# A two-layer graph kernel on one core: VectorE operands placed in PSUM, part of the last product moved into the node blocks

## The chip, the cores and the metric

The kernel runs on one core of a Trainium2 chip. The metric is the device time of the whole program in microseconds, lower is better. The core's engines are TensorE (PE, with its weight loads shown apart as PEld), VectorE (DVE), ScalarE (ACT), GpSimd (POOL) and SyncE (SP), and 16 DMA engines that they share. SBUF and PSUM are the two on-chip memories of 128 partitions; PE writes to PSUM, of which there are eight banks of 512 fp32 words per partition.

## The reference

Two message-passing layers over 6250 nodes of 160 features (64 scalars and 32 vectors of three) and 100,000 edges, all in fp32.

Layer 0 normalises the node rows (layer norm, then ReLU), gathers the row of the source of each edge, forms products with the four numbers of the edge, adds them up per node, and then forms in each node a full tensor product of the node's row with its sum (`uvw` products of 64x64x64, 64x32x32, 32x64x32 and 32x32x64) and a linear map; the input is added back. That gives y. Layer 1 normalises y again to h2, and does

```python
out_s = (einsum('eu,uo->eo', xs_e * es[:, None], W_ss) / sqrt(MUL_S) + einsum('eud,ed,uo->eo', xv_e, ev, W_vv) * ISQ3 / sqrt(MUL_V)) * ISQ2
out_v = (einsum('eu,ed,uv->evd', xs_e, ev, W_sv) * ISQ3 / sqrt(MUL_S) + einsum('eud,e,uv->evd', xv_e, es, W_vs) * ISQ3 / sqrt(MUL_V)) * ISQ2
messages = messages * sigmoid(edge_scalars @ W_rad.T + b_rad)
agg = segment_sum(messages, dst, num_segments=n)
h = x + agg
ys, yv = hs @ L_s / sqrt(MUL_S), einsum('nud,uv->nvd', hv, L_v) / sqrt(MUL_V)
```

with h2 as x, and the output is y plus this. The last product is linear, so the product of x + agg is that of x plus that of agg.

## The kernel before

Nodes are cut into NB = 49 blocks of 128. Edges are sorted by the block of their target, on the chip, and padded to windows of 256; two windows make a pair, and there are PAIRS = 220 pairs in each layer.

- **Ranks (VectorE, `ranks`, L506).** For each layer, keys are counted per block and given a place in the sorted order by a scan (L548, its first operand the constant `ones` in SBUF) and a predicated copy (L553) per block and part of the columns. The positions go to HBM. Between the two layers' ranks VectorE normalises the nodes (L580 to L599; `mean` and `rstd` are in SBUF).
- **Scatters (POOL, `scatter`, L408).** 782 indirect DMAs for each layer (L415) write the edges' records to their sorted places. SP loads pieces of records for layer 0, POOL itself for layer 1 (L425, L426).
- **Edges of layer 0.** POOL gathers the rows of a pair by four indirect DMAs (L449 into `xu`), up to five pairs ahead. ScalarE makes the keys (`dist`, L933) and scales the rows (L945). VectorE multiplies the rows with the edge's vector (L646, operand from `rw0` in SBUF), builds the one-hot matrices (`one_hot`, L617, from `iota` and `keyp` in SBUF), and adds the two sums of the pair before to the accumulator (L634). PE forms the sums (L1163).
- **Node blocks.** 49 blocks; VectorE forms the products (L728, L739, L747, L756, L762), PE turns them (`turn`, L1118, and L1230) and multiplies with the weights. For each block y is finished (L680 to L687), stored to `x2D` by SP (L350), normalised to `hb` (L707, L710), turned, copied to `hS` (L990), and `rows` (L1200) makes the table rows of layer 1 by two matmuls (L1202, L1203), which ScalarE copies (`copy_rows`) and SP stores. `rows(b-1)` stands in block b's program between the third and the fourth product of the turned blocks. POOL's scatters of layer 1 run beside this stage.
- **Edges of layer 1.** POOL gathers rows of 352 words (L449 into `tb`). VectorE: L858 (rows times the edge's vector, from `rw1`), L617, L865 (a sum over three), L827 (add of the sums of three pairs back), L833, L839, L827, L845 (messages times the gate `gt`). ScalarE: attributes (L1060), keys (L1063), L1082, the sigmoid (L1087, from PSUM to `gt`), scales (L1073). PE: flips (L1114), the gate's product (L1344), the sums (L1324).
- **Output (`output_pairs`, L240).** 49 blocks in turn, two in flight: VectorE adds the accumulator and `hS` (L897), PE flips the sum (L1114, `flip` is a matmul with the identity, `turn` a transpose) and forms the product (L1356, L1357), ScalarE copies, VectorE adds the row of x2 that SP has loaded (L893), SP stores 80 KB (L398).

The order on each engine is written out; loops run over pairs and over blocks, and engines wait for one another by counting semaphores.

## Time and profile before

| | us |
|---|---|
| median of 3 runs | 5143.87 |
| lowest and highest | 5098.26, 5165.8 |
| the profiled execution | 5144.9 |
| its span in the profile | 5143.2 |

| engine | busy us | share of the span |
|---|---|---|
| POOL | 3622.3 | 70% |
| DVE | 3371.4 | 66% |
| PE | 3032.4 | 59% |
| ACT | 1538.0 | 30% |

Shares are over stages that have different limits, so they don't say which engine sets the end. A row of the group view reads: line, engine, operation, output<-input by the program's names, partitions x elements, count | busy us, mean ns of one | idle time of the engine just before them, and what ended it. "issue" is time in which the engine waited for nothing that the profile shows. PEclk is the clock that TensorE was granted, as a share of 2.4 GHz; 0.5 is 1.2 GHz. In names, `acc` stands for all buffers that are cut from one large SBUF tile, and `ps` for PSUM.

### The profile page before, as it was taken

To read this page: it belongs to the slowest core of one execution; us is meant where nothing else is said; L and a number is where in the kernel's file an instruction comes from. 1 tells how busy PE (TensorE), PEld (TensorE's weight loads), DVE (VectorE), ACT (ScalarE), POOL (GpSimd) and SP (SyncE) were. 2 spreads that over 40 slices of the span, in tenths; PEclk is the share of its full clock that TensorE was granted. 3 is DMA by queue.
4 is the path that set the end of the run, shared out by engine and by line. 5 is a ranking of instruction groups with operands and counts; after the bars stand their busy time and mean duration, and the time that the engine had idled before them with its cause. 6 is when DMAs were issued, how large, how long until landed. Compare 5 with 4: busy or idle time off the path is not lost.

```text
span 5143.2 us, 56705 instructions
## 1 busy us (share of the span) xinstructions
PE 3032.4 (59%) x14598; PEld 1860.4 (36%) x14598; DVE 3371.4 (66%) x5385; ACT 1538.0 (30%) x4652; POOL 3622.3 (70%) x3420
## 2 busy tenths in 40 slices
PE   0030000005777777767888888888776677777779
PEld 0030000002222222224666656566544444444445
DVE  9959800005555555547999999999777677676751
ACT  0000000002333333333333333333254555554531
POOL 0787777777777777776777777777277777777740
PEclk9999999999999999999889999999799989899875
DMA  5020000003333333362111111111155555555571
GB/s 197 7 61 7 7 7 7 7 11 89 104 104 104 103 105 104 104 93 54 33 32 33 31 35 31 34 33 32 34 138 137 135 138 139 139 136 136 139 98 55
DMA packets 356674, 385.31 MB, mean 75 GB/s; under 512 B 213718, under 2 KB 276632, under 8 KB 356248
## 3 DMA queue, kind: packets, MB, share of 16 engines
q0 software_dynamic: 153760, 303.39, 24.0%
q1 hardware_dynamic: 178216, 60.22, 4.8%
q10 hardware_dynamic: 24656, 21.24, 1.3%
q8 instruction: 15, 0.25, 0.0%
q14 instruction: 27, 0.22, 0.0%
HBM read 326.47 MB, written 58.13 MB: 75 GB/s over the span
## 4 chain that ended last, share of the span: by engine, by line
PE 35%; POOL 17%; issue 15%; DVE 8%; DMA 2%; ACT 1%; DVEq 1%; ACTq 0%; POOLq 0%; SPq 0%
POOL acc L449 16%; PE ps L1163 15%; PE ps L1118 5%; PE ps L1250 4%; DVE room L617 3%; PE ps L1230 2%; PE ps L1211 2%; DVE acc L762 2%; PE ps L1284 1%; PE ps L1114 1%; DVE room L728 1%; PE ps L1356 1%; PE ps L1357 1%; DVE room L747 1%; DMA acc<-t_rows,acc 1%
## 5 line engine op out<-in xcount | busy, mean ns | idle before, releaser
L415 POOL DMA_INDIRECT sorted<-srec,spos x1564 | 1707.5, 1092 | 627.3 <-issue 475.8
L1163 PE MATMUL ps<-room 128*128 128x512 f32 x1760 | 821.6, 610 | 1110.8 <-DVE room L617 1110.8
L449 POOL DMA_INDIRECT acc<-t_rows,acc x880 | 984.5, 1119 | 359.3 <-issue 266.9
L449 POOL DMA_INDIRECT room<-h_rows,rw x880 | 877.3, 997 | 272.1 <-issue 251.3
L1163 PEld LDWEIGHTS ps<-room 128*128 128x128 f32 x1760 | 319.1, 191 | 1612.5 <-DVE room L617 1244.2
L1344 PE MATMUL ps<-ws,acc 128*128 128x448 f32 x880 | 474.7, 670 | 114.0 <-ACT acc L1082 114.0
L945 ACT ACTIVATE room<-room,rw 128x160 f32<-128x160 f32 x880 | 304.5, 416 | 780.4 <-DMA room<-h_rows,rw 780.4
L634 DVE TENSOR_TENSOR acc<-acc,ps 128x512 f32 x440 | 300.3, 683 | 286.9 <-PE ps L1163 286.7
L858 DVE TENSOR_TENSOR acc<-acc 128x768 f32<-128x768 f32 x220 | 212.3, 965 | 380.9 <-DMA acc<-t_rows,acc 379.7
L1118 PE MATMUL ps<-cst,room 128*128 128x128 f32 x1862 | 325.3, 303 | 123.5 <-DVE room L728 63.4
L646 DVE TENSOR_TENSOR room<-room,rw 128x768 f32<-128x768 f32 x220 | 211.4, 961 | 261.5 <-DMA room<-h_rows,rw 257.0
L607 DVE MEMSET acc<- 128x25088 f32 x1 | 21.0, 20965 | 526.4 <-issue 526.4
L756 DVE TENSOR_TENSOR room<-ps,room 128x1536 f32<-128x1536 f32 x196 | 342.4, 1747 | 7.6 <-PE ps L1211 7.6
L940 ACT ACTIVATE keyp<-rw,base 128x2 f32<-128x2 int32 x440 | 103.0, 281 | 812.0 <-DMA rw<-sorted 812.0
L762 DVE TENSOR_REDUCE acc<-room 128x96 f32<-128x1536 f32 x196 | 342.0, 1745 | 0.1
L1324 PEld LDWEIGHTS ps<-acc 128*128 128x128 f32 x1760 | 301.6, 214 | 109.6 <-issue 108.4
L1114 PE MATMUL ps<-cst,rwz 128*128 128x128 f32 x880 | 160.4, 308 | 281.4 <-DVE rwz L865 280.9
L1073 ACT ACTIVATE acc<-acc 128x160 f32<-128x160 f32 x880 | 302.6, 416 | 60.5 <-DMA acc<-t_rows,acc 60.2
L1118 PEld LDWEIGHTS ps<-cst,room 128*128 128x128 f32 x1862 | 214.5, 150 | 280.9 <-issue 120.1
L1324 PE MATMUL ps<-acc 128*128 128x160 f32 x1760 | 305.8, 322 | 1.0 <-DVE acc L845 1.0
L1230 PE MATMUL ps<-cst,room 128*128 128x128 f32 x1568 | 215.5, 295 | 102.1 <-DVE room L747 102.1
L728 DVE TENSOR_TENSOR room<-hS,room 128x512 f32<-128x512 f32 x392 | 257.0, 681 | 26.6 <-PE ps L1118 26.1
(145 smaller groups left out, 4981.0 us busy)
## 6 DMA issues: line engine op xcount, KB each, us to landing
sorted<-srec,spos POOLq DMA_INDIRECT x1564
sorted<-acc ACTq DMA_DIRECT2D x1, 14080.0 KB, 51.4
room<-h_rows,rw POOLq DMA_INDIRECT x880, 2.7
acc<-sorted SPq DMA_DIRECT2D x44, 320.0 KB, 3.8
acc<-t_rows,acc POOLq DMA_INDIRECT x880, 3.1
srec<-in_rec POOLq DMA_DIRECT2D x46, 272.0 KB
t_rows<-base SPq DMA_DIRECT2D x49, 176.0 KB
acc<-in_x SPq DMA_DIRECT2D x1, 3920.0 KB, 61.8
```

Source lines behind the costliest of these rows:

```text
L415: nc.gpsimd.indirect_dma_start(out=eD[l], out_offset=bass.IndirectOffsetOnAxis(ap=spos[:, h, k:k + 1], axis=0), in_=srec[:, h, k * r:(k + ...
L449: nc.gpsimd.indirect_dma_start(out=dst, out_offset=None, in_=table, in_offset=bass.IndirectOffsetOnAxis(ap=idx, axis=0)).then_inc(done, 16)
L728: v.tensor_tensor(pz[:, 512 * (j % 3):512 * (j % 3) + 512].rearrange("p (u v) -> p u v", v=S), hS[:, ds(b, 1), 8 * j:8 * j + 8].rearrange( ...
L756: v.tensor_tensor(mb.rearrange("p (k w j) -> p k w j", k=3, w=V), ps[:, u % 2, :].rearrange("p (o w j) -> p o w j", o=1, w=V).to_broadcast ...
L762: n.inc(v.tensor_reduce(o1[:, u * 3 * V:(u + 1) * 3 * V], mb.rearrange("p (c j) -> p c j", j=16), AX.X, ALU.add))
L945: last = a.activation(xu[:, t5, c, RH + 6 * V:XU], xu[:, t5, c, 3 * V:RH], ACT.Copy, scale=rw0[:, s, c, 5:6].bitcast(f32))
L1073: last = a.activation(sc[:, t2, c, :], tb[:, t5, c, 0:F], ACT.Copy, scale=rw1[:, s, c, 2:3].bitcast(f32))
L1118: return t.transpose(dst, src, ident)
L1163: last = t.matmul(ps[:, 2 * (s % 2) + w, :], oh[:, s % 2, 2 * w + cc, :], xu[:, t5, 2 * w + cc, 3 * V:XU], start=(cc == 0), stop=(cc == 1))
L1230: last = t.matmul(ps[:, 4, c * P:c * P + P], pz[:, k * 512 + c * P:k * 512 + c * P + P], ident, start=(k == 0), stop=(k == 2))
L1324: last = t.matmul(ps[:, 4 + s % 2, w * F:w * F + F], oh1[:, s % TSLOTS, 2 * w + cc, :], mg[:, s % 2, 2 * w + cc, :], start=(cc == 0), stop ...
L1344: last = t.matmul(ps[:, 2 * t2 + w, 0:GZ], azt[:, t2, w * P:(w + 1) * P], ws[:, WG:WG + GZ], start=True, stop=True)
```

## The change

- One of two SBUF operands of several VectorE instructions lies in PSUM: the constant of the scan, mean and rstd of the normalisation, the row 0 to 127 of the one-hot builds (`iota0`, `iota1`), the edge's vector in both layers (`rvec`, `evec`, copied there by ScalarE for every pair). The gate's sigmoid is written in place in PSUM and read from there by the product with the messages; `gt` goes.
- The waits follow: the product of layer 0 waits for the keys' semaphore, ScalarE's keys for the one-hot of two pairs before, the product of layer 1 for the attributes, the one-hot of layer 1 for the sums of three pairs before, the gate's matmul for the messages of two pairs before.
- The first two pieces of records of layer 1 are fetched by POOL before the gathers of layer 0 instead of after them.
- In each node block three more matmuls form y plus the final product of h2 in PSUM, and ScalarE copies that into `hS`, in place of the copy of `hb`. The table `x2D` with its stores and loads goes.
- The output stage turns the accumulator itself, four blocks at a time, and adds `hS` to the product; one store per group, 13 groups.

```diff
+        mean_ps, rstd_ps = ps[:, 7, 0:NB], ps[:, 7, 64:64 + NB]
+        iota0 = ps[:, 6, 3 * P:4 * P]
+        iota1 = [ps[:, 4 + b, 3 * P:4 * P] for b in range(2)]
+        rvec = [ps[:, 4 + b, 0:12].rearrange("p (c k) -> p c k", k=3) for b in range(2)]
+        evec = [ps[:, 6 + b, 2 * P:2 * P + 12].rearrange("p (c k) -> p c k", k=3) for b in range(2)]
...
             pool.wait_ge(filled[0], 16)
             scatter(0, False)
+
+            pool.wait_ge(pos_stored, 64)
+            for h in range(2):
+                pool.wait_ge(sent[0][h], 16 * CH * (PIECES // 2))
+                fetch(0, h, True)
             pool.wait_ge(h_stored, 48)
             pair_turns(pool, gather0)
...
-                            v.tensor_tensor_scan(run[h][:, 0:m], ones[:, 0:1].to_broadcast((P, m)), eq[h][:, 0:m],
+                            v.tensor_tensor_scan(run[h][:, 0:m], iota0[:, 1:2].to_broadcast((P, m)), eq[h][:, 0:m],
...
-            c.link(v.tensor_tensor(hS[:, :, :], xs, over(mean), ALU.subtract))
-            c.link(v.tensor_tensor(hS[:, :, :], hS[:, :, :], over(rstd), ALU.mult))
+            c.link(v.tensor_tensor(hS[:, :, :], xs, over(mean_ps), ALU.subtract))
+            c.link(v.tensor_tensor(hS[:, :, :], hS[:, :, :], over(rstd_ps), ALU.mult))
...
-                rr = rw0[:, s, :, 2:5].bitcast(f32).rearrange("p c (o k) -> p c o k", o=1).to_broadcast((P, 4, 2 * V, 3))
+                dve.wait_ge(key_done[0], q + 1)
+                rr = rvec[s % 2].rearrange("p c (o k) -> p c o k", o=1).to_broadcast((P, 4, 2 * V, 3))
...
-                dve.wait_ge(key_done[0], q + 1)
-                one_hot(oh[:, s % 2, :, :], keyp[:, t5, :], 4).then_inc(built[0], 1)
+                one_hot(oh[:, s % 2, :, :], iota0, keyp[:, t5, :], 4).then_inc(built[0], 1)
...
-                        dve.wait_ge(u_x2_out, b * 16)
+                        dve.wait_ge(t_mm, b)
...
-                v.tensor_tensor(mg[:, s % 2, :, :], mg[:, s % 2, :, :], gt[:, s % 2, :, :], ALU.mult).then_inc(msg, 1)
+                m = mg[:, s % 2, :, :].rearrange("p (w c) f -> p w (c f)", w=2)
+                v.tensor_tensor(m, m, ps[:, 2 * (s % 2):2 * (s % 2) + 2, 0:2 * F], ALU.mult).then_inc(msg, 1)
...
-                ev = rw1[:, s, :, 3:6].bitcast(f32).rearrange("p c (o d) -> p c o d", o=1).to_broadcast((P, 4, 2 * V, 3))
+                ev = evec[t2].rearrange("p c (o d) -> p c o d", o=1).to_broadcast((P, 4, 2 * V, 3))
+                dve.wait_ge(attr_in, q + 1)
...
-                one_hot(oh1[:, t5, :, :], keyp[:, t5, :], 4).then_inc(built[1], 1)
+                at_least(dve, summed[1], q - 2)
+                one_hot(oh1[:, t5, :, :], iota1[1 - t2], keyp[:, t5, :], 4).then_inc(built[1], 1)
...
+            for g in range(HG):
+                b, n = 4 * g, min(4, NB - 4 * g)
+                dve.wait_ge(f_mm, g + 1)
+                at_least(dve, f_out[g % 2], g // 2 * 16)
+                for h in range((n + 1) // 2):
+                    m = min(2, n - 2 * h)
+                    last = v.tensor_tensor(fo[g % 2][:, 2 * h * F:(2 * h + m) * F], ps[:, 4 + 2 * (g % 2) + h, 0:m * F],
+                                           hS[:, b + 2 * h:b + 2 * h + m, :].rearrange("p b f -> p (b f)"), ALU.add)
+                last.then_inc(f_done, 1)
...
-                at_least(act, built[0], q - TSLOTS + 1)
+                at_least(act, built[0], q - 1)
+                a.activation(rvec[s % 2], rw0[:, s, :, 2:5].bitcast(f32), ACT.Copy)
...
-            a.activation(hS[:, ds(b, 1), :].rearrange("p b f -> p (b f)"), hb, ACT.Copy).then_inc(h2_kept, 1)
...
+                a.activation(hS[:, ds(b, 1), :].rearrange("p b f -> p (b f)"), ps[:, 6, TM:TM + F], ACT.Copy)
                 a.activation(tS[:, 0:TM], ps[:, 6, 0:TM], ACT.Copy).then_inc(t_sb, 1)
...
+                a.activation(evec[t2], rw1[:, s, :, 3:6].bitcast(f32), ACT.Copy)
                 a.activation(rwz[:, t2, :, 6:23], rw1[:, s, :, 6:23].bitcast(f32), ACT.Copy).then_inc(attr_in, 1)
...
-                at_least(act, msg, q - 1)
-                a.activation(gt[:, t2, :, :].rearrange("p (w c) f -> p w (c f)", w=2), ps[:, 2 * t2:2 * t2 + 2, 0:2 * F],
-                             ACT.Sigmoid).then_inc(gate_done, 1)
+                g = ps[:, 2 * t2:2 * t2 + 2, 0:2 * F]
+                a.activation(g, g, ACT.Sigmoid).then_inc(gate_done, 1)
...
-                t.matmul(ps[:, 6, S:F], hT[0:V, P:2 * P], ws[0:V, WT + TM:WT + TM + 3 * V], start=False, stop=True).then_inc(t_mm, 1)
+                t.matmul(ps[:, 6, S:F], hT[0:V, P:2 * P], ws[0:V, WT + TM:WT + TM + 3 * V], start=False, stop=True)
+                x2 = ps[:, 6, TM:TM + F]
+                t.matmul(x2, ident, y, start=True, stop=False)
+                t.matmul(x2, hT[:, 0:P], ws[:, WF:WF + F], start=False, stop=False)
+                t.matmul(x2, hT[0:V, P:2 * P], ws[0:V, WF + F:WF + 2 * F], start=False, stop=True).then_inc(t_mm, 1)
...
-                at_least(pe, s_add, q - 1)
+                at_least(pe, msg, q - 1)
...
+            def sums_flipped(g):
+                n = min(4, NB - 4 * g)
+                a4 = acc1[:, 4 * g * F:(4 * g + n) * F].rearrange("p (b f) -> p b f", f=F)
+                at_least(pe, f_t_sb, g - 1)
+                for k in range(n):
+                    turn(ps[:, 2 * (g % 2), k * P:(k + 1) * P], a4[:, k, 0:P])
+                for k in range(n):
+                    last = turn(ps[0:V, 2 * (g % 2) + 1, k * P:(k + 1) * P], a4[:, k, P:F])
+                last.then_inc(f_t, 1)
+
+            def outputs(g):
+                n = min(4, NB - 4 * g)
+                pe.wait_ge(f_t_sb, g + 1)
+                at_least(pe, f_done, g - 1)
+                for k in range(n):
+                    dst = ps[:, 4 + 2 * (g % 2) + k // 2, k % 2 * F:(k % 2 + 1) * F]
+                    t.matmul(dst, fT[g % 2][:, k * P:(k + 1) * P], ws[:, WF:WF + F], start=True, stop=False)
+                    last = t.matmul(dst, fT[g % 2][0:V, (4 + k) * P:(5 + k) * P], ws[0:V, WF + F:WF + 2 * F],
+                                    start=False, stop=True)
+                last.then_inc(f_mm, 1)
```

## Rows read from the trace of the kernel before

**Rows 1.** Busy us and count by engine, PEclk, DMA share, GB/s, by stage.

```profile
132.00:1172.00 1040.00, 47.24 (x200) 42.00 (x200) 448.59 (x702) 12.36 (x27) 801.55 (x782) 1.00 0.08 14
1172.00:2335.00 1163.00, 812.55 (x1744) 315.63 (x1744) 623.42 (x871) 383.79 (x1310) 879.61 (x885) 1.00 0.42 102
2335.00:3715.00 1380.00, 1134.74 (x8738) 824.25 (x8738) 1256.08 (x1629) 483.22 (x1237) 956.48 (x870) 0.91 0.13 33
3715.00:4997.00 1282.00, 893.61 (x3520) 595.72 (x3520) 893.15 (x1761) 636.55 (x1980) 984.50 (x880) 0.89 0.55 135
4997.00:5143.00 146.00, 143.22 (x392) 81.84 (x392) 29.64 (x99) 20.80 (x98) 0.00 (x0) 0.51 0.19 55
```

**Rows 2.** POOL by line: 132:650, 660:1040, 2343:3625, 1176:2321, 3715:4973.

```profile
L415 POOL DMA_INDIRECT sorted<-srec,spos x369 | 406.2, 1101 | 243.9 <-DMA srec<-in_rec 132.1 <-issue 111.9
...
L415 POOL DMA_INDIRECT sorted<-srec,spos x302 | 289.1, 957 | 92.1 <-issue 92.1
...
L415 POOL DMA_INDIRECT sorted<-srec,spos x780 | 903.8, 1159 | 256.8 <-issue 237.4 <-DMA srec<-in_rec 19.4
...
L449 POOL DMA_INDIRECT room<-h_rows,rw x880 | 877.3, 997 | 272.1 <-issue 251.3 <-PE ps L1163 14.0 <-DMA rw<-sorted 6.7
...
L449 POOL DMA_INDIRECT acc<-t_rows,acc x880 | 984.5, 1119 | 359.3 <-issue 266.9 <-DMA acc<-sorted 91.3 <-DVE acc L833 1.1
```

**Rows 3.** Waits of POOL: total us, times, longest us.

```profile
POOL acc L449 <- issue: 266.9, 876, 0.3
POOL room L449 <- issue: 251.3, 812, 4.3
...
POOL acc L449 <- DMA acc<-sorted: 91.3, 3, 86.8
```

**Rows 4.** Timeline in layer 1: start us, us, instruction.

```profile
4200.46 0.82 DVE L845 TENSOR_TENSOR acc<-acc 128x640 f32<-128x640 f32 x1
...
4200.60 1.50 POOL L449 DMA_INDIRECT acc<-t_rows,acc  x1 [0.30 <-issue]
...
4204.26 0.31 DVE L827 TENSOR_TENSOR acc<-acc,ps 128x160 f32 x1
...
4204.40 0.95 POOL L449 DMA_INDIRECT acc<-t_rows,acc  x1 [0.30 <-issue]
4204.48 0.55 DVE L833 TENSOR_TENSOR acc<-acc 128x384 f32<-128x384 f32 x1
```

**Rows 5.** VectorE's groups by shape, 512 elements.

```profile
L634 DVE TENSOR_TENSOR acc<-acc,ps 128x512 f32 x440 | 300.3, 683 | 286.9 <-PE ps L1163 286.7
...
L617 DVE TENSOR_TENSOR room<-cst,keyp 128x512 f32<-128x512 f32 x220 | 150.5, 684 | 0.0
```

**Rows 6.** Busy time as in rows 1, end of the layer-1 gathers.

```profile
4960.00:4980.00 20.00, 13.81 (x48) 9.37 (x48) 12.03 (x25) 8.39 (x26) 9.23 (x9) 0.80 0.99 111
```

**Rows 7.** VectorE's groups by shape from 132 to 650 us.

```profile
L548 DVE TENSOR_TENSOR_SCAN acc<-cst,acc 128x612 f32<-128x612 f32 x99 | 147.8, 1493 | 3.5
L553 DVE COPY_PREDICATED acc<-acc 128x612 f32<-128x612 int32 x99 | 82.3, 832 | 0.0
```

**Rows 8.** Node blocks: a wait of VectorE; timeline of PE in one block.

```profile
DVE room L739 <- PE ps L1118: 27.3, 22, 1.3
...
3038.81 0.60 PE L1202 MATMUL ps<-ws,rwz 128*128 128x256 f32 x2
3039.34 0.46 PE L1203 MATMUL ps<-ws,rwz 32*128 32x96 f32 x2
3039.73 0.66 PE L1250 MATMUL ps<-room 128*64 128x128 f32 x8
```

**Rows 9.** Timeline: eight turns in a node block; PE in the output.

```profile
3651.23 1.57 PEld L1118 LDWEIGHTS ps<-cst,room 128*128 128x128 f32 x8 [1.50 <-issue]
...
5040.17 0.90 PE L1356 MATMUL ps<-ws,room 128*128 128x160 f32 x2
5041.00 0.89 PE L1357 MATMUL ps<-ws,room 32*128 32x160 f32 x2
5041.82 1.36 PE L1114 MATMUL ps<-cst,room 128*128 128x128 f32 x4
5043.11 0.90 PE L1356 MATMUL ps<-ws,room 128*128 128x160 f32 x2
```

121 lines of the change are left out of this document (39 added, 82 removed).

## The prediction

> **What bounds the kernel now.** I read the busy time by stage first, with the stretches cut where POOL changes its work [rows 1]. The reader is to see five stages. (a) 132 to 1172 us: POOL issues the 782 scatters of layer 0 while VectorE ranks the keys. (b) 1172 to 2335: 880 gathers and the edge products of layer 0. (c) 2335 to 3715: the 49 node blocks, with VectorE at 1256 of 1380 us, and beside them the 782 scatters of layer 1. (d) 3715 to 4997: 880 gathers and the edges of layer 1. (e) 4997 to 5143: the output, with PE at 143 of 146 us and a granted clock of 0.51, which is its 1.2 GHz level.
>
> Then I asked POOL what it waits for. In (a), (b) and (d) it waits for nobody: its groups show about 0.3 us of issue between two instructions and no long releaser [rows 2]. The one long wait, 86.8 us, stands in front of (d): POOL had ended its scatters and node blocks were still running [rows 3]. So POOL sets the end of (a), (b) and (d), node blocks set (c), and PE sets (e). In (c) POOL has 87 us to spare; what it gains there is worth nothing.
>
> Last, POOL's own instructions. One scatter takes 957 ns when VectorE does nothing (660 to 1040 us), 1101 while it ranks and 1159 beside the node blocks; a gather takes 997 in (b) and 1119 in (d) [rows 2]. The instruction is the same, so something stretches it. The timeline shows what [rows 4]: the gather that starts at 4200.60, 0.14 us into the product L845, takes 1.50 us; the one at 4204.40 takes 0.95. The product ends at 4201.28, 0.68 us after that start, and the gather is 0.55 us too long. L845 has both inputs in SBUF. The gather of 4204.40 starts inside L827 (4204.26 to 4204.57), one of whose inputs is in PSUM, and isn't stretched. So a POOL instruction that comes to its reading under a VectorE instruction with two SBUF inputs stands until that is over.
>
> **Part 1, the operands in PSUM.** The change puts one of the two inputs of these VectorE instructions in PSUM: the scan L548, the normalisation L597 and L598, the products L646, L858 and L845, and both one-hot builds (L617). VectorE itself neither gains nor loses: 512 elements take 684 ns with both inputs in SBUF (L617) and 683 with one in PSUM (L634) [rows 5]. I cost the move at nothing on VectorE. ScalarE gets one small copy per pair (rvec, evec), 440 in all; it is busy 384 of 1163 us in (b) and 637 of 1282 in (d) [rows 1], which hides them.
>
> *Stage (d).* Unhindered, a gather costs 0.95 us [rows 4] plus 0.30 of issue (266.9 over 876 [rows 3]) = 1.25, so 880 cost 1100; they now take 1257 (984.5 busy, 359.3 idle, less the 86.8 in front) [rows 2, 3]. That is 157 us. Back off it: L833 still has two SBUF inputs. 0.8 gathers a us, 220 instructions of 0.55 us and half of that as the mean wait give 0.8 x 220 x 0.15 = 27 us; since the gather at 4204.40 gets in just ahead of it, as the cycle repeats itself, I take half, 13. And in the last 70 us (some 50 gathers) the DMA engines are at 0.99 [rows 6], so 50 x 0.18 = 9 us don't come. 157 - 13 - 9 = **135**. Bounds: 0 if the wait has another cause, 157.
>
> *Stage (b).* 997 minus 950 [rows 2, 4], times 880, is 41 us; both colliding kinds (L646, L617) are changed. 3 us are lost in its own slow tail: **38**. Two fetches for layer 1 move in front of this stage: four POOL issues of under 0.6 us, inside the 4.3 us for which POOL waits there for the first records [rows 3]. They cost nothing; without that cover 2.3 us. They spare 19 us of waiting ahead of the scatters in (c) [rows 2], where POOL has slack.
>
> *Stage (a).* 369 scatters up to 650 us are each 1101 - 957 = 144 ns long, 53 us in all. The predicated copy L553 stays in SBUF: 99 of 832 ns, so 0.8 x 99 x 0.35 = 28 us stay [rows 7], and about 5 for its short form and the weights' product; the scans and the normalisation give back the rest, **20**. Nothing to 53 is the range. POOL doesn't run dry now (the 132.1 us of waiting are all ahead of its first scatter), and it will come to the second part of the positions, after 170 scatters, at most 170 x 0.14 = 24 us earlier.
>
> **The waits that this adds.** L646 now waits for ScalarE's key copies of its pair and L858 for ScalarE's attributes; both are made a pair ahead, before ScalarE waits for this pair's rows, and the first adds of the pair before queue behind them. ScalarE's keys of layer 0 wait for the one-hot two pairs back instead of five, which is done. The one-hot of layer 1 waits for the sums of the pair three back, for which the add just behind it waits anyway. The gate's matmul waits for L845 instead of L839 of two pairs back; VectorE has done both before the L865 on which that same matmul depends. L680 waits for a matmul of the block before instead of a store. I cost all of them at nothing. If L858 did wait for attributes, POOL has five slots of rows between itself and VectorE, so up to about 0.9 us a pair (5.0 against VectorE's 4.1, 893 us over 220 [rows 1]) would stay hidden.
>
> **Part 2, the node blocks.** Each adds three matmuls behind L1203: the identity times y and two for the final product. It takes away the store of y and the wait on it, and the copy of hb to hS becomes one from PSUM of the same length. Is PE on the path? VectorE waits 22 times, 27.3 us in all, before L739 for the last turn (L1118) of the block before; the new matmuls stand ahead of that turn in PE's order [rows 8]. So nearly all of their time shows. L1202 (256 columns) is 0.53 us from its start to that of L1203, and that one (32 rows, 96 columns) 0.39 to the next instruction [rows 8]. Two of 160 columns on 128 rows and one on 32 rows are about 0.28 + 0.28 + 0.42 = 0.98 us, a little less where VectorE is the later one: 0.95 x 48 = **-45**. Bounds: 0 if VectorE's own work covered them, -80 if they ran at the low clock, at which L1356 to L1357 is 0.83 apart [rows 9].
>
> **Part 3, the output.** The sum of acc and hS, the load of x2 and 49 small stores go; 13 groups of up to four blocks remain. Only PE counts: 2.94 us per block now, of which 0.84 and 0.82 for the two matmuls (L1356, L1357) and 1.29 for two flips (L1114) [rows 9]. The matmuls stay. The flips become turns, which leave one record each where a flip leaves two: at the low clock eight turns keep the weight load busy 1.57 us, a pitch of 0.22 each [rows 9]. Per block 1.66 + 0.44 = 2.1 us, 49 x 0.84 = 41, and about 1 for the start: **42** if the clock stays at its low level. If it rose, 2.1 would be near 1.1 and the gain some 50 us more. PE runs without a break there now and is still granted 0.51 [rows 1], so I keep the low level. The Trainium skill, "TensorE: Matmul & The Clock Gate", section "Part 4: PE-mode transpose", states that transposes don't raise the clock as matmuls do; no run here shows that yet. By this rule the stage would be the same 103 us.
>
> **The sum.** 135 + 38 + 20 - 45 + 42 = 190 us off the profiled execution, which took 5144.9 us (span 5143.2) and is 1 us from the median of the runs, 5143.87. That gives **4955 us**. 2% (103 us) is about what a measurement of this kernel can tell from no change: its three runs reach from 5098 to 5166.
>
> **The rivals.** *The gathers wait for something else.* Against it is the match of 0.55 us in rows 4. For it: every gather of (d) moves longer rows than one of (b), and that could be part of 1119 against 997. Then parts 2 and 3 remain: 5145 + 45 - 42 = 5148. The Trainium skill, "SBUF — State Buffer", section "Who interferes with whom", speaks on both sides: a VectorE instruction with two SBUF inputs contends with a GpSimd instruction that reads SBUF, yet it infers that descriptor generation is not held up by a tensor_tensor. By the second sentence this rival holds; by the first the sum does. The trace sides with the first, 1.50 against 0.95 us.
>
> *L833 takes the place of the others.* VectorE starts a pair when its rows land, so POOL and VectorE are locked in phase. Now the gather of 4204.40 starts 0.08 us ahead of L833 [rows 4]. If in the new cycle it falls just behind, each pair loses up to 0.5 us: 220 x 0.45 = 99 instead of 13, so 5041.
>
> *Node blocks at the low clock.* The granted clock of (c) is 0.91. More PE work between the same waits may shift it. If twice as many blocks ran low, at some 3 us each, another 50 us, and the matmuls at 80 instead of 45: 5040.
>
> *The output's clock rises* to its upper level, as part 3 has it: 4905.
>
> *Slower.* PE at the low clock becomes the bound of (d). PE is busy 894 us in (d) at a mean clock of 0.89, so near one fifth of the time at the low level: 4.06 us a pair, which is 3.3 at the high and 6.6 at the low one, against the 5.0 in which POOL will deliver a pair. If (d) ran low throughout, it would take 220 x 6.6 = 1452 us instead of 1122: 5285. The kernel is slower than now from 220 x 3.3 x (1 + f) = 1122 + 190, which is f = 0.8 of the stage; nothing in the change starves PE there.
>
> **How the numbers follow.** Forecast 0.62; output clock up 0.12; L833 0.10; node clock 0.08; other cause 0.05; slower 0.03. The two at 5040 lie on the edge of 5041, and half of them counts as faster: faster 0.62 + 0.12 + 0.09 = 0.83, within 2% 0.09 + 0.05 = 0.14, slower 0.03. The range takes in 4905 and the two at 5040, with a little room at each end: 4885 to 5050.
>
> **What would show it.** The mean of a gather in (d) near 0.96 us and in (b) near 0.95, and of a scatter at 660 to 1040 us still 957; scatters beside the node blocks still about 1159, since their products keep both inputs in SBUF; stage (d) near 1145 us; node blocks a mean 0.9 us longer with more waiting before L739; an output of about 106 us at a clock of 0.5. It is wrong if gathers in (d) stay over 1.05 us, if L833 becomes the instruction under which long gathers start, or if PE, not POOL, paces the pairs.

## The result, and the profile after

The kernel after takes 4915.51 us in the median of 4 runs (4912.64 to 4954.28), the kernel before 5146.69 in the median of 4 (5098.26 to 5165.8). The ratio is 0.959, with a 95% interval of 0.952 to 0.967: faster by 4%. The profiled execution has a span of 4910.9 us, against 5143.2 of before. That is 232 us less, where 190 were forecast.

First the stages of the kernel after, cut where POOL changes its work. Columns are us from the span's start, length, busy us and count of PE, PEld, DVE, ACT and POOL, granted clock, DMA share, GB/s.

```profile
132.00:1174.00 1042.00, 47.06 (x200) 41.90 (x200) 466.28 (x703) 12.36 (x27) 803.19 (x782) 0.59 0.08 14
1174.00:2340.00 1166.00, 817.69 (x1755) 317.87 (x1756) 613.00 (x879) 416.82 (x1540) 844.58 (x896) 0.99 0.42 103
2340.00:3708.00 1368.00, 1135.08 (x9022) 838.36 (x9020) 1250.64 (x1623) 472.99 (x1227) 921.59 (x860) 0.96 0.11 30
3708.00:4830.00 1122.00, 814.41 (x3464) 545.62 (x3464) 873.88 (x1730) 645.64 (x2178) 839.30 (x880) 0.94 0.61 153
4830.00:4911.00 81.00, 70.39 (x350) 47.78 (x350) 25.40 (x57) 20.62 (x50) 0.70 (x1) 0.96 0.29 65
```

Against [rows 1] the first three stretches have hardly moved in length. The fourth is 1122 us, where before needed 1257 from its first gather to its last. The output's clock is 0.96 instead of 0.51.

POOL's groups of the same kernel come next, first layer 0's scatters, then both gather stages. Columns are line, operation, tiles, count, busy us, mean ns, and idle time with what ended it.

```profile
L401 POOL DMA_INDIRECT sorted<-srec,spos x782 | 803.4, 1027 | 370.2 <-issue 238.1 <-DMA srec<-in_rec 132.1
...
L422 POOL DMA_INDIRECT room<-h_rows,rw x880 | 831.8, 945 | 317.8 <-issue 292.2 <-DMA rw<-sorted 17.3 <-PE ps L1140 8.2
...
L422 POOL DMA_INDIRECT acc<-t_rows,acc x880 | 840.0, 955 | 397.5 <-issue 259.9 <-DMA acc<-sorted 115.9 <-DVE acc L815 21.7
```

Beside [rows 2], the gather of layer 1 fell from 1119 to 955 ns and that of layer 0 from 997 to 945. Both are at the unhindered 950. In layer 0, however, the idle time rose from 272.1 to 317.8 us and took the gain back.

The stages can be cut more exactly at POOL's own instructions: (a) from the first scatter of layer 0 to the end of the last, (b) and (d) the same for the gathers, (c) between the two gather stages, (e) from the last gather to the end. The small rest between (a) and (b) is called the gap. The first 15 to 28 us or so of (e) are the last pairs of layer 1, which are still worked off; from then on PE is busy in the output. All runs of this study, in us, with the mean scatter or gather in ns:

| kernel | chip | (a), mean | gap | (b), mean | (c) | (d), mean | (e) |
|---|---|---|---|---|---|---|---|
| before | - | 1040, 1025 | 4 | 1145, 997 | 1394 | 1257, 1119 | 171 |
| after | - | 1042, 1027 | 6 | 1146, 945 | 1382 | 1122, 955 | 80 |
| e1 layer 1 in SBUF | 4 | 1082, 1063 | 44 | 1350, 945 | 1991 | 1420, 1098 | 80 |
| e2 one-hot first | 4 | 1081, 1061 | 46 | 1294, 945 | 1980 | 1491, 948 | 120 |
| e3 the same on before | 4 | 1103, 1095 | 26 | 1287, 1040 | 1928 | 1421, 1118 | 163 |
| e4 no node product | 4 | 1078, 1058 | 46 | 1355, 948 | 1930 | 1484, 953 | 84 |
| e5 flips in output | 6 | 1080, 1070 | 47 | 1347, 945 | 1879 | 1484, 950 | 98 |
| e6 turns on before | 6 | 1102, 1098 | 7 | 1333, 986 | 1862 | 1375, 1131 | 118 |
| e7 scan output in PSUM | 6 | 1055, 1027 | 106 | 1345, 948 | 1886 | 1471, 954 | 127 |
| e8 rows behind last turn | 6 | 1077, 1056 | 39 | 1345, 948 | 1953 | 1472, 955 | 117 |
| e9 e2 and e7 together | 13 | 1056, 1026 | 114 | 1295, 945 | 1966 | 1495, 950 | 121 |
| e10 messages in SBUF | 13 | 1076, 1062 | 42 | 1350, 948 | 1941 | 1463, 1021 | 80 |
| e11 lead of three | 5 | 1040, 1026 | 6 | 1160, 945 | 1378 | 1218, 967 | 115 |
| e12 lead, pauses, order | 5 | 1042, 1028 | 6 | 1119, 946 | 1447 | 1212, 962 | 115 |

One thing has to be said before the experiments can be read. On chips 4, 6 and 13 the kernel before itself took 6106, 5973 and 6115 us, and on chip 5 it took 5101. The two profiles compared above are like chip 5. On the other three, whole engines stand still for several us again and again (last section). Totals of e1 to e10 are therefore compared only with before on the same chip, and mechanisms are read from stretches and instructions that the standing doesn't touch. The kernel after itself was traced only once, beside before; where a run is set against it, (a) and (c) show whether the chip is of its kind (e11: 1040 and 1378 us against 1042 and 1382).

### The profile page after: what moved, and what is told of

Same layout as the page of the kernel before. It is cut to its first block, busy times and chain, and to the rows that moved or that the text cites. A ratio compares the mean times of both kernels' runs of the same rounds, so it can differ in the third digit from the quotient of the medians.

```text
span 4910.9 us, 56344 instructions
## 1 busy us (share of the span) xinstructions
PE 2885.7 (59%) x14794; PEld 1792.5 (36%) x14794; DVE 3349.6 (68%) x5316; ACT 1569.7 (32%) x5020; POOL 3409.6 (69%) x3420
## 4 chain that ended last, share of the span: by engine, by line
PE 35%; POOL 27%; issue 18%; DVE 15%; DMA 3%; ACT 1%; DVEq 1%; ACTq 0%; POOLq 0%; SPq 0%
PE ps L1140 16%; POOL sorted L401 16%; POOL acc L422 11%; PE ps L1095 5%; PE ps L1231 4%; DVE acc L613 3%; PE ps L1211 3%; DVE room L596 3%; DMA acc<-t_rows,acc 2%; DVE acc L741 2%; PE ps L1192 1%; DVE room L707 1%; DVE acc L496 1%; PE ps L1265 1%; DVE room L726 1%
## 5 line engine op out<-in xcount | busy, mean ns | idle before, releaser
L401 POOL DMA_INDIRECT sorted<-srec,spos x1564 | 1685.0, 1077 | 608.6 <-issue 476.5
L422 POOL DMA_INDIRECT acc<-t_rows,acc x880 | 840.0, 955 | 397.5 <-issue 259.9
L422 POOL DMA_INDIRECT room<-h_rows,rw x880 | 831.8, 945 | 317.8 <-issue 292.2
L613 DVE TENSOR_TENSOR acc<-acc,ps 128x512 f32 x440 | 300.1, 682 | 470.5 <-PE ps L1140 470.4
L916 ACT ACTIVATE ps<-rw 128x12 f32<-128x12 f32 x220 | 40.7, 185 | 1424.0 <-DMA rw<-sorted 802.5
L1325 PE MATMUL ps<-ws,acc 128*128 128x448 f32 x880 | 427.9, 612 | 114.4 <-ACT acc L1061 114.4
L842 DVE TENSOR_TENSOR acc<-acc,ps 128x768 f32<-128x768 f32 x220 | 209.8, 954 | 245.9 <-issue 164.1
L735 DVE TENSOR_TENSOR room<-ps,room 128x1536 f32<-128x1536 f32 x196 | 342.2, 1746 | 1.3 <-PE ps L1192 0.9
L1305 PEld LDWEIGHTS ps<-acc 128*128 128x128 f32 x1760 | 278.2, 199 | 94.5 <-issue 93.3
L1095 PEld LDWEIGHTS ps<-cst,room 128*128 128x128 f32 x1862 | 200.0, 142 | 257.6 <-issue 98.0
L1305 PE MATMUL ps<-acc 128*128 128x160 f32 x1760 | 287.1, 308 | 1.0 <-DVE acc L828 1.0
L626 DVE TENSOR_TENSOR room<-room,ps 128x768 f32<-128x768 f32 x220 | 208.7, 949 | 85.3 <-DMA room<-h_rows,rw 36.9
L1211 PEld LDWEIGHTS ps<-cst,room 128*128 128x128 f32 x1568 | 223.0, 227 | 110.5 <-DVE room L726 110.5
```

The costliest lines, as they stand in the source:

```text
L401: nc.gpsimd.indirect_dma_start(out=eD[l], out_offset=bass.IndirectOffsetOnAxis(ap=spos[:, h, k:k + 1], axis=0), in_=srec[:, h, k * r:(k + ...
L422: nc.gpsimd.indirect_dma_start(out=dst, out_offset=None, in_=table, in_offset=bass.IndirectOffsetOnAxis(ap=idx, axis=0)).then_inc(done, 16)
L613: v.tensor_tensor(a, a, ps[:, 2 * (s % 2) + w, :], ALU.add).then_inc((added_first, added)[w][0], 1)
L735: v.tensor_tensor(mb.rearrange("p (k w j) -> p k w j", k=3, w=V), ps[:, u % 2, :].rearrange("p (o w j) -> p o w j", o=1, w=V).to_broadcast ...
L1095: return t.transpose(dst, src, ident)
L1211: last = t.matmul(ps[:, 4, c * P:c * P + P], pz[:, k * 512 + c * P:k * 512 + c * P + P], ident, start=(k == 0), stop=(k == 2))
```

## The experiments

**Are the operands the cause in layer 1? (e1, e10)** In the kernel after:

```diff
-    a.activation(g, g, ACT.Sigmoid).then_inc(gate_done, 1)
+    at_least(act, msg, q - 1)
+    a.activation(gt[:, t2, :, :].rearrange(...), g, ACT.Sigmoid).then_inc(gate_done, 1)
-    v.tensor_tensor(m, m, ps[:, 2 * (s % 2):2 * (s % 2) + 2, 0:2 * F], ALU.mult)
+    v.tensor_tensor(m, m, gt[:, s % 2, :, :].rearrange(...), ALU.mult)
 # e1 alone, not e10:
-    ev = evec[t2].rearrange(...)
+    ev = rw1[:, s, :, 3:6].bitcast(f32).rearrange(...)
-    one_hot(oh1[:, t5, :, :], iota1[1 - t2], keyp[:, t5, :], 4)
+    one_hot(oh1[:, t5, :, :], iota, keyp[:, t5, :], 4)
```

> The kernel after, with the second operand of VectorE's three instructions of layer 1 (message product, edge-vector product, one-hot build) back in SBUF; the sigmoid is written to an SBUF buffer again. Everything else, ScalarE's small copies included, is as after. Theory (a POOL gather that starts under a VectorE instruction with two SBUF inputs stands until that is over): the stage of the layer 1 gathers goes from 1122 us back to about 1257, the mean gather from 955 to about 1120 ns, the kernel from 4915 to about 5050. Rival (the 135 us came from something else in the edit, such as the waits or the output's order): the stage stays at 1122 us and the kernel at 4915.

> The kernel after with only the message product's factor (the sigmoid's output) back in SBUF; the edge-vector product and the one-hot build keep their PSUM operands. It is VectorE's longest of the three, 0.95 us. Theory: gathers that start under it are stretched again, the others aren't: the mean gather of layer 1 between 955 ns (none stretched) and 1098 ns (all three back in SBUF), about 1010 to 1040, and the median pair period above 5.00 us. Rival (the small copy by ScalarE and the product's own place count, not its operand): 955 ns as in the kernel after. On a chip with a kernel before of about 5145 us the stage would take 1160 to 1220 us against 1122.

POOL's group of layer 1's gathers, in e1, e10 and e4 (whose layer 1 is as in the kernel after):

```profile
L423 POOL DMA_INDIRECT acc<-t_rows,acc x880 | 966.5, 1098 | 1243.4 <-DMA acc<-sorted 792.5 <-issue 270.8 <-DVE acc L816 180.1
```

```profile
L423 POOL DMA_INDIRECT acc<-t_rows,acc x880 | 898.2, 1021 | 1297.4 <-DMA acc<-sorted 732.4 <-DVE acc L816 303.5 <-issue 261.4
```

```profile
L422 POOL DMA_INDIRECT acc<-t_rows,acc x880 | 838.4, 953 | 1369.8 <-DMA acc<-sorted 725.5 <-DVE acc L815 346.6 <-issue 297.7
```

The gather takes 953 ns with one operand of each of the three instructions in PSUM, 1021 with the message product's back in SBUF, and 1098 with all three back. Between e1, e10 and the kernel after only these operands, the sigmoid's buffer and its wait differ. The instruction that VectorE runs 0.1 us after a gather's start says more. In e1 the gathers are longer than 950 ns each by 63 us in sum under the edge-vector product, 46 under the message product and 24 under the one-hot build. In e10 it is 40 us under the message product and none under the other two, but 23 us under L816, which always had two SBUF inputs and holds up gathers for only 0.2 us in e1 and 7.5 in the kernel after (there L815). So the cause named by the prediction is shown, and a third of what e10 shows is the move to another holder, not the operand that was put back. The stage did not follow on chip 4: 1420 us in e1 against 1484 and 1491 in e4 and e2, so there the shorter gathers went with a longer stage. The whole of e1 is level with before (ratio 1.003, 0.998 to 1.008), and e10 is at 1.012 (1.003 to 1.022). The expected 5050 us says nothing here.

**What holds stage (b)? (e2, e3)** In the kernel after, and with its own operands in the kernel before:

```diff
-                if behind:
-                    add0(q - 1, s - 1, 0, numbers0[t5][0])
                 one_hot(oh[:, s % 2, :, :], iota0, keyp[:, t5, :], 4).then_inc(built[0], 1)
                 if behind:
+                    add0(q - 1, s - 1, 0, numbers0[t5][0])
                     add0(q - 1, s - 1, 1, numbers0[t5][1])
```

> The kernel after, with one exchange in VectorE's order of layer 0: the one-hot build of pair q stands ahead of both adds of pair q-1 instead of between them. Theory (stage (b) is paced by a ring of three: one-hot 0.68 us, TensorE's eight records 3.70 us, first add 0.61 us, in all 5.19 to 5.20 us a pair, because one-hot q+1 stands behind the add that waits for TensorE's pair q): the exchange takes the add out of the ring, POOL becomes the bound at about 1.25 us a gather, the stage goes from 1146 us to 1100 to 1110, the kernel to about 4873. Rival (POOL or the rows' landing sets the pace and VectorE only seems to wait): stage (b) stays at 1146, the kernel at 4915.

> The kernel before, with the same exchange in VectorE's order of layer 0. If POOL with gathers of 997 ns is as slow as the ring (880 x 1.30 = 1144 us against 220 x 5.19 = 1142), the exchange alone gives nothing: stage (b) 1140 to 1145 us, the kernel 5145 or a few us less. Rival (the ring was the only bound): stage (b) falls to about 1100 us here too, the kernel to about 5105.

What the expectation calls a ring is in the timeline of the kernel after (start, duration, instruction):

```profile
1700.29 3.70 PE L1140 MATMUL ps<-room 128*128 128x512 f32 x8 [1.49 <-DVE room L596]
...
1704.13 0.69 DVE L613 TENSOR_TENSOR acc<-acc,ps 128x512 f32 x1 [2.44 <-PE ps L1140]
1704.74 0.68 DVE L596 TENSOR_TENSOR room<-ps,keyp 128x512 f32<-128x512 f32 x1
...
1705.48 3.70 PE L1140 MATMUL ps<-room 128*128 128x512 f32 x8 [1.49 <-DVE room L596]
```

PE's sums of one pair end, the add L613 that waited 2.44 us for them runs, only then comes the one-hot L596, and PE's next sums start with its end: 5.19 us around. 220 turns of it are 1142 us, as many as POOL needed with gathers of 997 ns.

With the exchange, the time from one pair's first gather to the next (median of 219 differences of the starts) is 5.00 us in e2 and in e9, against 5.20 to 5.26 in e1, e4, e7, e8 and e10. The stage is 1294 us against 1350 and 1355 on the same chip. So this ring, and not POOL, held stage (b) of the kernel after. In e3 the median is 5.44 us (5.27 in e6, which has the old order), with a mean gather of 1040 ns: 4 x (1.04 + 0.30) = 5.36. By these medians the gathers hold the pair there, and the exchange alone doesn't shorten it. In total e2 is at 1.005 of before (1.002 to 1.009) and e3 at 0.986 (0.980 to 0.993). So e3 gained, where nothing or a few us were expected, and its stage is shorter than that of e6 on another chip (1287 against 1333). The medians don't explain that, and before's stages weren't traced on this chip. That only both edits together gain fits the pair periods; by the totals it is not shown.

**What do the three matmuls in a node block cost? (e4, e8)** In e4 the last three matmuls of rows(b) are left out and h2 is copied to hS. In e8 the call moves:

```diff
-                    if j == 2 and not first:
+                    if j == 4 and not first:
 ...
                         rows(b - 1)
 # ScalarE's copies of its results:
-                    if j == 5 and not first:
+                    if j == 6 and not first:
                         copy_rows(b - 1, isinstance(b, int) and b == 1)
```

> The kernel after without the three matmuls that the node blocks got (identity times y and the two of the final product); ScalarE copies h2 to hS as before. Left out of the output is y plus the product of h2 with the final weights. Theory: a node block at the full clock goes from about 27.3 us back to 26.1, 48 x 1.2 = 57 us, and VectorE's wait for the last turn goes back from 1.28 us a block to about half a microsecond. If the blocks of some 30 us at a low clock, which only the kernel before has, hang on the emptier TensorE, about 9 of them return and eat 30 of the 57: stage (c) 1310 to 1340 us and the kernel 4860 to 4885. Rival (the low blocks came from the store of y, which is gone in this kernel too): none return, stage (c) 1310 and the kernel 4858. If the three matmuls are hidden: 1368 and 4915.

> The kernel after, with TensorE's five matmuls of rows(b-1) issued behind the last four turns of the block instead of ahead of the last two groups of them, and ScalarE's copies of their results one step later. Theory (VectorE's 1.28 us of waiting before each product that follows the last turn is the time of matmuls ahead of that turn): the wait goes, a block takes 26.0 to 26.2 us instead of 27.3, stage (c) 48 x 1.2 = 58 us less, the kernel 4857. Rival (the time only moves to the wait at the start of the next block, or the clock of TensorE falls in some blocks as in the kernel before): less than 25 us come, the kernel above 4890.

Node blocks beside POOL's scatters take 44 to 54 us in the mean on these chips. When POOL is done, 22 to 28 blocks are left that run undisturbed, and they can be read. Taken from one SCALAR_TENSOR_TENSOR of VectorE to the next, these last blocks are:

- kernel after's form (e1, e5, e7, e10): mean 27.2 to 27.3 us, nearly all between 26.8 and 27.7
- e4, without the three matmuls: mean 27.5 us, from 25.4 to 30.3
- kernel before's form (e6, e3): means 27.9 and 27.4 us, from 24.0 to 30.6
- e8: mean 27.3 us

Stretches of about one block each, of e4 and then of e5 (same columns as the stages above):

```profile
4036.00:4062.00 26.00, 20.99 (x180) 15.30 (x180) 25.29 (x34) 9.78 (x26) 0.00 (x0) 1.00 0.03 10
4062.00:4088.00 26.00, 22.39 (x180) 16.88 (x179) 25.30 (x33) 9.51 (x25) 0.00 (x0) 0.93 0.03 10
4088.00:4119.00 31.00, 27.75 (x186) 20.03 (x186) 26.04 (x37) 10.49 (x26) 0.00 (x0) 0.78 0.03 8
```

```profile
4226.00:4253.00 27.00, 23.37 (x184) 17.52 (x184) 25.11 (x33) 9.25 (x26) 0.00 (x0) 0.94 0.03 10
4253.00:4281.00 28.00, 23.99 (x190) 18.14 (x189) 25.70 (x36) 9.99 (x26) 0.00 (x0) 0.94 0.03 9
4281.00:4307.00 26.00, 21.37 (x179) 15.34 (x178) 24.69 (x32) 9.06 (x25) 0.00 (x0) 1.00 0.03 10
```

Without the matmuls, blocks of 26.0 us stand beside blocks of 30 us in which the granted clock is 0.78. With them no block is that slow, and none but the last is that fast. The matmuls do cost 0.8 to 1.2 us in a block at the higher clock; the slow blocks that go with them pay it back. That the slow blocks hang on these matmuls and not on the store of y is shown, since e4 has no store either. Why the clock behaves so is not: the runs only show which kernel has them.

In e8, the waits of VectorE over its undisturbed blocks (total us, times, longest), then the same in e5:

```profile
DVE room L659 <- PE ps L1198: 30.7, 24, 1.5
DVE room L735 <- PE ps L1192: 10.8, 25, 0.4
DVE room L707 <- PE ps L1211: 3.8, 13, 0.4
```

```profile
DVE room L718 <- PE ps L1095: 30.7, 23, 2.5
DVE room L659 <- PE ps L1198: 9.1, 22, 0.6
```

The wait before L718 is gone. 1.3 us a block of it now stand before L659, which waits for PE's first product of the next block. The block is as long as before; the rival of the expectation holds. These matmuls cost their time wherever they stand in the block.

**What sets the output's clock? (e5, e6)** In e5 both calls of turn in sums_flipped are flip; in e6 both calls of flip in the kernel before's sum_t are turn.

> The kernel after, with the eight turns per group of the output as flips (matmuls with the identity as the moving operand, two records each) and nothing else changed. The output of the kernel after takes 80 us at a granted clock of 1.00, that of the kernel before 146 at 0.51. Theory A (the clock rose because of the groups of four, which leave TensorE no short waits): the clock stays at 0.9 to 1.0, the stage gets longer only by the flips' second record, some 49 x 0.2 = 10 us: about 90 us, the kernel 4925. Theory B (the clock rose because turns took the place of flips): the clock falls to about 0.5 and the stage takes some 49 x (1.66 + 1.29) = 145 us, the kernel 4980.

> The kernel before, with turns instead of flips in the output and nothing else. Theory A (groups of four raised the clock): still 0.51, the stage gets 49 x (1.29 - 0.44) = 42 us shorter, about 105 us of output, the kernel 5103; less if the chain sum, flip, copy, product of one block then sets the pace. Theory B (turns raised it): the clock rises to 0.9 or more and the output takes 60 to 75 us, the kernel 5065.

The stretch from the last gather to the end, in e5, e6 and e2 (whose output is that of the kernel after):

```profile
5970.00:6068.00 98.00, 91.78 (x460) 63.92 (x460) 26.76 (x59) 22.71 (x58) 0.51 (x1) 0.92 0.21 51
```

```profile
5812.00:5930.00 118.00, 109.85 (x346) 70.47 (x346) 41.26 (x123) 27.43 (x118) 0.00 (x0) 0.56 0.31 75
```

```profile
6025.00:6145.00 120.00, 111.97 (x366) 73.26 (x364) 27.89 (x62) 23.63 (x61) 0.06 (x1) 0.60 0.14 38
```

Flips in groups of four reach 0.92; turns block by block stay at 0.56. So turns aren't needed for the high mean, and theory B falls. But the third row shows that theory A isn't whole either: the same output as in the kernel after ran at 0.60 and took 120 us. Over all traces with groups of four, (e) is 80 to 98 us in five (after, e1, e4, e5, e10) and 115 to 127 in six (e2, e7, e8, e9, e11, e12), with one and the same code but for e5. These means hide when the clock moved. Two stretches of e4's output and then one of e2's:

```profile
6044.00:6091.00 47.00, 46.72 (x249) 32.17 (x249) 8.00 (x18) 11.60 (x22) 0.00 (x0) 1.00 0.20 63
6092.00:6110.00 18.00, 15.63 (x42) 9.43 (x39) 2.10 (x5) 1.49 (x4) 0.00 (x0) 0.50 0.19 59
```

```profile
6051.00:6145.00 94.00, 91.76 (x264) 59.00 (x264) 10.99 (x25) 11.07 (x22) 0.00 (x0) 0.50 0.13 43
```

In every output, the clock falls from 1.00 to 0.50 once for good. In the six long ones it falls 5 to 8 us after PE's last break (of 1 us), in after, e1 and e10 56 us after it, which is 1 to 2 us before PE's end, in e4 47 us after it and 16 us before the end, in e5 9 us before the end. What sets the moment is not shown. The three outputs block by block (before, e3, e6) all fall at the start, which is too few to say that they always do. e6 shows the part of the turns at the low level: 118 us against 171 and 163, some 49 less.

**Why did the scatters of (a) not gain? (e7)** In the kernel after, 95 scatters start under the predicated copy L530 and are together 46 us longer than 950 ns each; in the kernel before it was 10 us under the copy L553 and 24 under the scan L548. The edit:

```diff
-        run = [early(EC) for _ in range(2)]
+        pf = ps.rearrange("p b f -> p (b f)")
+        run = [pf[:, 2560 + 640 * h:2560 + 640 * h + EC - EARLY * CH] for h in range(2)]
-        iota0 = ps[:, 6, 3 * P:4 * P]
+        iota0 = ps[:, 7, 3 * P:4 * P]
```

> The kernel after, with the scan's output buffers (which the predicated copy reads) in PSUM, so that the predicated copy has one SBUF input besides the rank it keeps. In the kernel after 95 of the scatters of stage (a) start under the predicated copy and are 46 us too long in sum; the stage runs from 132.7 to 1174 us. Theory (its data operand is the second SBUF read that holds POOL up): the scatters beside the ranking shrink from 1.02 us in the mean to about 0.96, stage (a) gets 35 to 50 us shorter, the kernel 4870 to 4880. Rival 1 (mask and kept output are two SBUF operands by themselves, or the instruction holds POOL whatever it reads): no change, 4915. Rival 2 (scans and compares then meet POOL in another phase): the extras move to them and less than 20 us come.

POOL's scatters of stage (a) in e7, and in e8, which keeps run in SBUF:

```profile
L402 POOL DMA_INDIRECT sorted<-srec,spos x782 | 803.0, 1027 | 384.9 <-issue 252.3 <-DMA srec<-in_rec 132.5
```

```profile
L401 POOL DMA_INDIRECT sorted<-srec,spos x782 | 825.5, 1056 | 382.9 <-issue 251.1 <-DMA srec<-in_rec 131.8
```

Under the predicated copy the excess fell from 27 us in 88 scatters to 2.6 us in 53, and (a) became 22 us shorter; e9, with the same edit, agrees (1056 us). So the copy, too, holds POOL as long as its data come from SBUF. The mean scatter of e7 is still 1027 ns and not the 960 that was expected. About half of what is left stands in scatters during which VectorE runs nothing: 142 of them are over 100 ns too long, and in sum they lose 29 us. e8 has 111 such scatters (23 us), the kernel after on its own chip none. The stage behind it gave this back on chip 6: POOL then waited 84.8 us for VectorE's positions instead of 4.8, so (a) and gap together are 1161 us against 1116. VectorE is late there because it stands still itself. In the kernel after, on the chip of its profile, the gap is 6 us. What the edit gives there wasn't run.

**Two edits together (e9)** are those of e2 and e7.

> The kernel after with two of the edits together: layer 0's one-hot build ahead of both adds, and the scan's output in PSUM. On a chip whose kernel before takes about 5145 us: stage (b) from 1146 to about 1105 us (the pair period from 5.19 to 5.00), stage (a) from 1042 to about 1020, since VectorE is ahead there, so 4855 us against 4915. On a chip whose kernel before takes about 6000 to 6100 us, with engines standing still for 4 to 20 us now and then: stage (b) 50 to 60 us shorter than the 1345 to 1355 us there, the median pair period 5.00 us, and stage (a) shorter by 20 us but followed by the wait of 85 us for VectorE's positions, so about the same total as the kernel after there, 6080 to 6130 us.

Stage (b) took 1295 us with a median pair of 5.00, against 1350 in e10; (a) took 1056 with a gap of 114. Each edit did in its stage what it had done alone; what the two give on a chip like that of the kernel after wasn't run. The total is 6172 us, 1.012 of before (1.003 to 1.021).

**POOL's lead (e11, e12)** was meant for the standing engines, but the chip of these two runs has none, so that question stayed open. They gave something else.

```diff
-                at_least(pool, summed[0], q - TSLOTS + 1)
+                at_least(pool, summed[0], q - 2)
-                at_least(pool, v_add, q - TSLOTS + 1)
+                at_least(pool, v_add, q - 2)
 # e12 besides: the exchange of e2, and in scatter(), layer 1:
+                        if l == 1 and k in (6, 12):
+                            pool.wait_ge(sent[l][h], j * (16 * CH) + 16 * k)
+                            pool.sem_inc(pool_go, 1)
```

> The kernel after; POOL fetches rows at most three pairs ahead of their use in both gather stages instead of five. On the chips of runs e1 to e10, where the kernel before takes about 6000 to 6100 us, TensorE, ScalarE or VectorE stand still for 7 to 9 us about once in five pairs although what they wait for is done, and in the layer 1 stage most of these stretches end 2 to 3 us after POOL has filled its slots and stopped issuing. Theory (the standing engine can't go on while POOL issues back to back, so a POOL with more slots and shorter gathers keeps it standing longer): with two pairs less to fetch the stretches shrink by several us, stage (d) falls from 1471 to 1495 us to about 1200 to 1300, stage (b) from 1345 to about 1250 to 1300, and the kernel from about 6120 to 5800 to 5950. Rival (their length has nothing to do with POOL's lead): (d) 1470 to 1500, (b) 1345 to 1355, and the kernel as after there, 6080 to 6150. On a chip with a kernel before of 5145 us: no change, 4915.

> The run before, and with it two pauses in each piece of 17 scatters of layer 1 (POOL waits for the scatters issued so far after the 6th and the 12th, some 1.8 us each as at the end of a piece) and the one-hot build of layer 0 ahead of both adds. Theory: node blocks beside the scatters take 44 to 54 us in the runs before and 27.2 when the scatters are over; with a pause every 7.6 us the standing stretches there, up to 20 us now, end within 10 us, a block beside the scatters takes 32 to 40 us, stage (c) falls from about 1880 to 1990 us to 1500 to 1700; the order gives some 40 us of stage (b); in all 5450 to 5700 us, faster than both kernels on such a chip. Rival: stage (c) stays at 1880 to 1990 us and the kernel above 5900. On a chip with a kernel before of 5145 us the pauses cost 92 x 1.8 = 166 us of POOL's time, of which 115 us are slack: about 4915 + 50 - 40 = 4925 us.

Stages (d) and (e) of e11:

```profile
3719.00:4937.00 1218.00, 845.29 (x3484) 563.44 (x3484) 879.10 (x1741) 653.54 (x2185) 849.64 (x879) 0.93 0.57 141
4937.00:5050.00 113.00, 107.53 (x332) 69.72 (x331) 19.93 (x46) 17.26 (x38) 0.00 (x0) 0.56 0.13 39
```

e11 takes 5050 us, 0.985 of before (0.975 to 0.995), and not 4915. Two pairs less of lead cost 96 us in (d), a median pair of 5.35 instead of 5.00, and 14 in (b). VectorE frees a pair's slot only one pair later, so three slots are two in effect. The low clock of the output adds 35. My "no change" was wrong: three slots are too few for the 1122 us (four wasn't run).

e12 repeats the ring's test on a chip without standing engines. Two of its waits of VectorE in (b) are now:

```profile
DVE room L629 <- DMA room<-h_rows,rw: 461.9, 218, 7.8
DVE acc L616 <- PE ps L1142: 5.1, 7, 1.8
```

In the kernel after the same list had 466.6 us for PE and 30.2 for the rows. VectorE now waits for POOL's rows and no longer for PE, and (b) is 1119 us against 1160 in e11: 41 us from the exchange. The pauses cost 69 us of (c). In total it is 5042 us, 0.984 of before (0.974 to 0.994). The kernel after with only the exchange should take some 40 us less than the kernel after on such a chip; that is worked out from e11 and e12 and was not run.

## Why the prediction was right, and where it wasn't

4915.51 lies in the range of 4885 to 5050, 40 us under the forecast of 4955. By its terms:

- **Stage (d), 135 us: 1257 to 1122 = 135.** The step with the mean gather, 0.95 of duration and 0.30 of issue, came out as worked. e1 and e10 show the cause. That the term is met to the microsecond is luck: 22 us were set aside, 13 for holds by L833 and 9 for the tail. The holds under L815 (the L833 of before) are 7.5 us in 48 gathers, and POOL waited 21.7 us for L815 because its slots were full, 14.7 of them at once at 4791 us, with the DMA engines at 0.98.
- **Stage (b), 38 us: none.** The gathers did become 52 ns shorter, as forecast. What failed is the reading that POOL sets the end of (b) because it waits for nobody. POOL and the ring of one-hot, sums and add were equally long, 1141 and 1142 us, and a POOL with equal partners shows no waits. The sign stood in [rows 5]: L634 waits 286.7 us for L1163. I used that row only for its duration. e2 and e12 show the ring; 41 us came once it was cut.
- **Stage (a), 20 us: none** (1040 to 1042). The step failed that left the predicated copy its old share: 46 us of excess instead of 10. The scan gave back 21 us (24 to 3) and the normalisation some 14, and the copy took 36. POOL and VectorE move in step there, and a hold that is taken away lets the next one catch the same scatters. On chips 4 and 6, where VectorE stands still now and then, the kernel after's form has a shorter (a), 1077 to 1082 us against 1102 and 1103, but it waits longer in the gap: together 1124 to 1127 against 1129 on chip 4, and 1116 and 1127 against 1109 on chip 6.
- **Node blocks, -45 us: +12** (1394 to 1382). Only 2 of the 12 are the blocks: 48 of them, from the first y to the last, took 1309.9 and 1307.7 us. The rest is the end of layer 0 (VectorE's last add came 29.3 us after the last gather and now 17.8). The mechanism held: VectorE waits about 1.3 us before L718 in every block (58.7 us in 47), and undisturbed blocks at the higher clock went from 26.0 to 26.8 or more. The term missed the other side. The kernel before has nine blocks of 29 to 31 us at a clock of about 0.77, and these vanished; mean clock 0.91 to 0.96. I had the clock as a rival in the wrong direction.
- **Output, 42 us: 91** (171 to 80). The sum per block was right for the low clock: in e12 eight turns take 1.76 us and each of the four pairs of matmuls 1.66, 2.1 us a block, and the six traces at that level need 115 to 127 us in all, 44 to 56 less than 171. The profiled execution had the high one, as the rival said, which gave 91 in place of about 50. The step that kept the low level rested on before's mean of 0.51 with a busy PE; the same busy PE is granted 1.00 for 56 us in the kernel after. The Trainium skill, "TensorE: Matmul & The Clock Gate", section "Part 4: PE-mode transpose", has transposes not raise the clock. Here turns and flips in groups both reached 0.92 or more, and the turns in groups were also granted 0.60, so the choice between them doesn't decide it. No run has turns without matmuls between them, so the page's rule by itself was not tested.

That the sum was close is luck in part: two terms that didn't come (58 us) stand against two that came out better (57 us for (c), of which some 10 are the end of layer 0, and 49). The cause of the largest term, and with it the sign, was right for its reason. The likeliest case had the output at its low clock, so the profiled execution met a case that was given 0.12; that the timed runs reach from 4913 to 4954 fits two levels some 40 us apart, but their clocks by stage aren't known.

On the chips with standing engines the change doesn't gain. No unchanged kernel after ran there, but e5 differs from it by the flips alone, less than 20 us of 6081, and is 1.025 of before (1.015 to 1.035). The prediction knew nothing of this. Its slower case has a slip: 4.06 us a pair at a mean clock of 0.89 is about 3.6 us at the higher level and 7.2 at the lower, not 3.3 and 6.6. Nothing came of it, since PE didn't pace the pairs of (d).

## What to carry to other kernels

An engine that waits for nobody may still have an equal: before a shorter instruction is credited with its whole gain, work out the longest ring of the other engines over one period, and take the difference. When holds on POOL are removed one by one, don't count the whole gain while another remains that it can meet in its rhythm: that one may take the place, as the copy did in (a), or not, as L815 in (d). A term that hangs on TensorE's granted clock deserves both of its values in the sum, and the mean over a stage should be split to see when the clock moved.
